# A four-layer network on one core: the last attention layer gets SP-only transfers of eight per half batch, evictions first on ScalarE, two residual buffers and q/k products at the head of TensorE's slots

## The reference

```python
h = ((xg - mu) * rsqrt(var + EPS)).reshape(B, C, N) * norm_w[None, :, None] + norm_b[None, :, None]
qkv = (h.transpose(0, 2, 1) @ qkv_w.T + qkv_b).reshape(B, N, 3, nh, hd)
q, k, v = (qkv[:, :, 0], qkv[:, :, 1], qkv[:, :, 2])
attn = softmax(einsum('bnhd,bngd->bnhg', q, k) * hd ** (-0.5))
o = einsum('bnhg,bngd->bnhd', attn, v).reshape(B, N, C)
return x + (o @ proj_w.T + proj_b).transpose(0, 2, 1)
```

## Time and profile before

| | |
|---|---|
| median of 3 runs | 2309.95 us (2307.72 to 2318.79) |
| the profiled execution's own time | 2301.12 us |
| its span in the trace | 2299.3 us |
| last layer in the trace | about 1810 to 2299 us |
| steady batches 1 to 6 of it | 1868.68 to 2228.66 us |
| granted TensorE clock, whole span | 0.928 |

### The profile page before, as it was taken

The page is one execution under the profiler, slowest core; times in us unless marked ns, Lnnn a source line. Parts: engine busy times, 40 slices in busy tenths (PEclk is TensorE's granted clock), DMA queues, the critical chain, the costliest instruction groups (busy, mean ns, idle before and its releaser), DMA issues.

```text
span 2299.3 us, 36501 instructions
## 1 busy us (share of the span) xinstructions
PE 1999.9 (87%) x12212; PEld 1020.5 (44%) x12212; DVE 1521.9 (66%) x2315; ACT 829.6 (36%) x1546; POOL 1028.1 (45%) x437
## 2 busy tenths in 40 slices
PE   6998786799999999999999999999999777777775
PEld 2443233345544545545545445445543444344442
DVE  6766557787766766767677677677661366666666
ACT  0253220014544544444444444444456222222220
POOL 0242200025543644545455444453546166666666
PEclk7899898789999999999999999999999888889886
DMA  6200020250231232133123213303310201111111
GB/s 212 56 2 0 1 108 8 47 170 12 65 75 42 53 94 49 28 94 75 35 61 75 55 42 75 76 20 75 75 38 2 77 24 61 61 61 61 42 42 58
DMA packets 89410, 132.54 MB, mean 58 GB/s; under 512 B 57925, under 2 KB 58231, under 8 KB 89207
## 3 DMA queue, kind: packets, MB, share of 16 engines
q1 hardware_dynamic: 70486, 128.31, 20.0%
q10 hardware_dynamic: 18720, 1.64, 0.6%
HBM read 44.83 MB, written 25.17 MB: 30 GB/s over the span
## 4 chain that ended last, share of the span: by engine, by line
PE 71%; DVE 13%; issue 4%; ACT 4%; DMA 3%; ACTq 3%; SPq 2%; POOL 1%; POOLq 0%; DVEq 0%
PE AV L636 11%; PE S L623 11%; PE RB L607 11%; PE S L607 5%; PE SUM L646 4%; PE RB L675 4%; PE RB L871 3%; DVE MX L1274 3%; ACTq L1087 3%; PE AV L886 2%; SPq L438 2%; PE RB L922 2%; PE RB L752 2%; PE RB L692 2%; DVE NMH L1282 1%
## 5 line engine op out<-in xcount | busy, mean ns | idle before, releaser
L1274 DVE TENSOR_REDUCE MX<-RB 128x1 f32<-128x512 f32 x783 | 515.1, 684 | 88.5 <-PE RB L607 79.5
L1001 ACT ACTIVATE PR<-S 128x512 f32<-128x512 f32 x640 | 356.3, 597 | 582.3 <-PE S L623 563.0
L1173 POOL TENSOR_TENSOR ACC<-PR 128x1024 f32<-128x1024 f32 x72 | 170.3, 2373 | 761.1 <-ACT PR L1001 759.1
L623 PE MATMUL S<-QS,KS 98*128 98x512 f32 x1152 | 469.8, 459 | 17.5 <-issue 8.3
L1173 POOL TENSOR_TENSOR ACC<-ACC,PR 128x1024 f32<-128x1024 f32 x152 | 360.0, 2372 | 200.3 <-ACT PR L1001 191.7
L607 PE MATMUL RB<-KS,QS 96*128 96x512 f32 x783 | 393.7, 525 | 29.8 <-DVE MX L1274 18.9
L1001 ACT ACTIVATE X<-S 128x512 f32<-128x512 f32 x512 | 283.5, 598 | 281.1 <-PE S L623 273.6
L607 PEld LDWEIGHTS RB<-KS,QS 96*128 96x128 f32 x783 | 245.1, 318 | 249.2 <-DVE MX L1274 151.9
L623 PEld LDWEIGHTS S<-QS,KS 98*128 98x128 f32 x1152 | 221.9, 198 | 218.6 <-issue 93.3
L1274 DVE TENSOR_REDUCE MX<-S 128x1 f32<-128x512 f32 x369 | 251.6, 682 | 32.4 <-PE S L607 27.0
L607 PE MATMUL S<-KS,QS 96*128 96x512 f32 x369 | 186.3, 505 | 12.6 <-DVE MX L1274 8.1
(11 more groups left out here) (234 smaller groups left out, 2114.7 us busy)
## 6 DMA issues: line engine op xcount, KB each, us to landing
X<-out_y SPq DMA_DIRECT2D x32, 1024.0 KB, 4.9
out_y<-X SPq DMA_DIRECT2D x24, 1024.0 KB, 4.1
QS<-HI SPq DMA_DIRECT2D x144, 128.0 KB, 2.5
KS<-HI SPq DMA_DIRECT2D x144, 128.0 KB, 2.5
QS<-LO SPq DMA_DIRECT2D x72, 128.0 KB, 2.5
KS<-LO SPq DMA_DIRECT2D x72, 128.0 KB, 2.5
X<-in_x SPq DMA_DIRECT2D x8, 1024.0 KB, 8.2
WO<-WO ACTq DMA_DIRECT2D x128, 8.0 KB
```

The costliest lines, as they stand in the source:

```text
L623: mm(ST[:, (H * s + h) % BANKS, :], KS[par][:, h, P * mt:P * mt + P], QS[par][:, h, HALF * half:HALF * half + HALF], start=True, stop=True ...
L1001: nc.scalar.activation(exps(i, s, pair)[:, HALF * one:HALF * one + HALF], ST[:, (H * s + h) % BANKS, :], ACT.Exp, scale=1.0 if i is None e ...
L1173: nc.gpsimd.tensor_tensor(ACC[:, pair, :], so_far, exps(i, s, pair), ALU.add).then_inc(pool_used, 1)
L1274: nc.vector.tensor_reduce(out=MX[:, h, t, half:half + 1], in_=bank(), op=ALU.max, axis=AX.X).then_inc(ring_free, 1)
```

## The change

On SP the transfers of a half batch are now eight, with 128 source and 16 target partitions each, and ScalarE starts none; the order of tokens in `scores3` follows. The residual has a second buffer (LATC, memory of the layers before), used in turn, loaded and stored in two transfers each. TensorE runs `front_qk` first in each slot; ScalarE runs `keep_qk`, `keep_o`, `keep_v` first and only then `exp3` and `keep_p`. `group_sums` stands in slots 3 and 5 and `group_stats` in slots 4 and 6 (before: 3 and 4 on both), and GpSimd's `norm_factors` in slot 7 (before: 6).

```diff
-        P_DMAS = 2 * PAIRS
+        P_DMAS = PAIRS
...
+            def load_xres(b):
+
+                for t in range(CT):
+                    load(XRES3[b % 2][t], out_d[b, :, t], xres_in)
+
             sp.wait_ge(y_ready, B)
+            load_xres(1)
             load(out_d[B - 1], XRES, y_out)
             sp.wait_ge(y_out, 16 * B)
-            load(XRES, out_d[0], xres_in)
+            load_xres(0)
...
-                for g in range(PAIRS):
-                    cg, pair = g // PAIRS, g % PAIRS
-                    load(PTK[TOK * g:TOK * g + TOK, st].rearrange("t h j g -> t (h j g)"),
-                         SC[st][64 * cg:64 * cg + 64, pair].rearrange("p j g -> p (j g)"), p_in3)
+                for pair in range(PAIRS):
+                    load(PTK[2 * TOK * pair:2 * TOK * pair + 2 * TOK, st].rearrange("t h j g -> t (h j g)"),
+                         SC[st][:, pair].rearrange("p j g -> p (j g)"), p_in3)
...
                 share(b, 0)
+                if b > 1:
+                    sp.wait_ge(y_out, 16 * (B + CT * (b - 1)))
+                    load_xres(b)
                 share(b, 1)
...
-                        first = P * st + 64 * cg + TOK * pair
+                        first = P * st + 2 * TOK * pair + TOK * cg
...
+                    if b < B - 1:
+                        for unit in FRONT_UNITS[k]:
+                            front_qk(b + 1, unit)
                     if 0 <= n < TILES:
                         transpose3(n)
                     if b > 0 and k in (1, 2, 5, 6):
                         project3(b - 1, k // 4, 0 if k in (1, 5) else 1)
-                    if b < B - 2 and k in (3, 4):
-                        group_sums(k - 3, B + b + 2)
+                    if b < B - 2 and k in (3, 5):
+                        group_sums((k - 3) // 2, B + b + 2)
                     if b < B and k == 3:
                         scores3(b, 1)
                     if b < B - 1:
-                        for unit in FRONT_UNITS[k]:
-                            front_qk(b + 1, unit)
...
-                    if b < B and k in (0, 4) and (b, k) != (0, 0):
-                        exp3(b, k // 4)
-                    if b < B and k in (0 if b == 0 else 1, 5):
-                        share(b, k // 4)
-                    if b < B and k in (3, 7):
-                        keep_p(b, k // 4)
+                    if b < B - 1:
+                        for unit in FRONT_UNITS[k]:
+                            keep_qk(b + 1, unit)
                     if 0 <= n < TILES:
                         keep_o(n)
                     if b < B - 1:
-                        for unit in FRONT_UNITS[k]:
-                            keep_qk(b + 1, unit)
                         keep_v(b + 1, k)
+                    if b < B and k in (0, 4) and (b, k) != (0, 0):
+                        exp3(b, k // 4)
+                    if b < B and k in (3, 7):
+                        keep_p(b, k // 4)
```

More of the change, by code:

```diff
@@ L330, in program @@
                for n in range(2)]
+        XRES3 = [[XRES[:, t] for t in range(CT)], [LATC[t] for t in range(CT)]]
         O3 = [ENC[:, C * n:C * n + C] for n in range(2)]
@@ L545, in share @@
                     sp.wait_ge(p_kept3, 2 * (b - 1) + st + 1)
-                for g in range(PAIRS):
-                    cg, pair = g // PAIRS, g % PAIRS
-                    load(PTK[TOK * g:TOK * g + TOK, st].rearrange("t h j g -> t (h j g)"),
-                         SC[st][64 * cg:64 * cg + 64, pair].rearrange("p j g -> p (j g)"), p_in3)
+                for pair in range(PAIRS):
+                    load(PTK[2 * TOK * pair:2 * TOK * pair + 2 * TOK, st].rearrange("t h j g -> t (h j g)"),
+                         SC[st][:, pair].rearrange("p j g -> p (j g)"), p_in3)
             def store(b):
                 sp.wait_ge(y_ready, B + b + 1)
[L554 to L557, removed]
+                for t in range(CT):
+                    load(out_d[b, :, t], XRES3[b % 2][t], y_out)
             next_xin(1)
@@ L567, in _ @@
             store(B - 1)
-            sp.wait_ge(y_out, 16 * 2 * B)
+            sp.wait_ge(y_out, 16 * (B + CT * B))
         @block.tensor
@@ L1077, in exp3 @@
                                      scale=float(D) ** -0.5).then_inc(e_done3, 1)
[L1079 to L1088, removed]
             def keep_p(b, st):
@@ L1213, in _ @@
                     n = MT * b + k - 3
-                    if b < B - 2 and k == 6:
+                    if b < B - 2 and k == 7:
                         norm_factors(B + b + 2, GNS3, GNB3)
@@ L1620, in residual3 @@
                 if st == 0 and o == 0:
-                    dve.wait_ge(xres_in, 16 * (B + b + 1))
-                cols = super_tile(XRES[:, o, :], st)
+                    dve.wait_ge(xres_in, 16 * (B + CT * max(b + 1, 2)))
+                cols = super_tile(XRES3[b % 2][o], st)
                 nc.vector.scalar_tensor_tensor(out=cols, in0=quarters(src), scalar=BP3[:, o:o + 1], in1=cols,
@@ L1638, in _ @@
                         residual3(b - 1, k // 4, 0 if k in (2, 6) else 1)
-                    if b < B - 2 and k in (3, 4):
-                        group_stats(k - 3, B + b + 2)
+                    if b < B - 2 and k in (4, 6):
+                        group_stats((k - 4) // 2, B + b + 2)
                     if 0 <= n < TILES:
```

## The result

The changed kernel takes 2284.48 us (median of 4 runs, 2280.91 to 2288.11) against 2308.84 (2306.68 to 2318.79) for the kernel before on the same chip: a ratio of 0.9883, with a 95% interval of 0.9838 to 0.9928. It is faster, but by 24 us where 58 were forecast, and lies half a microsecond above the upper end of the range. The profiled execution took 2280.91 us, with a span of 2279.1 and a mean granted clock of 0.923.

What follows compares the result with a forecast made beforehand. Bound: waits in a TensorE–ScalarE loop, with ScalarE's transfer starts on it. Six batches save 53.4 us, batch 0 5, last iterations 2, start costs 2.5: 57.9 off 2301.12 gives 2243, with 8.8 for the median 2252; range 2226 to 2284.

Steps and rivals of the forecast that it cites:

- what the transfers cost on SP: SP's eight transfers a half batch: 7.7 us, or 13.4 if issuing doubles; data wanted 14 and 12.5 us after `weigh`; nothing charged.
- rival C: SP's transfers take three times as long to start and reach GpSimd late: 5 us a batch, 2282 us; chance 0.07.
- D: Rival: q/k units ahead of transposes and projections delay VectorE's projections by 13.7 us a batch, 2392 us; chance 0.05.
- E: Rival: no change, the delays of D and the transfers' gain cancel, 2310 us; chance 0.04.
- `front_v` of slot 0: TensorE's slot 0: waits for `keep_o` behind the group norm, then runs at half clock, charged 2.3 us.
- rival A: Clock doesn't fall at slot 0: `front_v` and a q/k unit give back 2.3 us a batch, 2238 us; chance 0.15.
- the rest of the walk round a batch: Adding up the engines' steps from one `centre` of slot 0 to the next: 51.1 us a batch instead of 60.0.
- slot 4 with its group statistics (0.8): VectorE's slot 4, where `group_stats` now stands: the statistics were charged 0.8 us.
- the bank wait: TensorE's slot 5: `group_sums` waits for the projection's bank until VectorE's residual of slot 6, delaying `front_v` by 1.9 us.
- rival B: Close waits of slots 4, 5 and 6 bring a second half-clock stretch: 3.7 us a batch, 2274 us; chance 0.2.
- `keep_p`: ScalarE's copy between the eviction after slot 7's `front_v` and the group norm, charged 0.2 us.
- the start of the layer: Last layer's start: loading the second residual buffer ahead of layer three's last store costs 2.5 us, bounds 0 and 5.

Runs made afterwards that it cites:

- e7: Kernel before with only the transfers changed: eight from SP, none from ScalarE, old orders and single residual buffer; 2290.55 us, 0.992 of before.
- e14: Changed kernel with `group_sums`, `group_stats` and `norm_factors` back in their old slots; 2244.57 us, 0.9722 of before.
- e8: Kernel before with only the new orders of TensorE's q/k units and ScalarE's evictions, ScalarE still starting transfers; 2316.37 us, 1.0038 of before.
- e10: Changed kernel with `group_stats` working in PSUM and `keep_p` first in ScalarE's slots 3 and 7; 2241.42 us, 0.9687 of before.
- e12: e6 with three tiny VectorE instructions added in slot 1, two with one SBUF input, one with two; 2239.25 us, 0.9689 of before.
- e1: Changed kernel with `group_stats` working in PSUM, so its square has no two SBUF inputs; 2264.64 us, 0.9783 of before.
- e9: Changed kernel with only the second `group_sums` and `group_stats` moved to slot 4; 2255.55 us, 0.9787 of before.
- e2: Changed kernel with `keep_p` first in ScalarE's slots 3 and 7; 2279.79 us, 0.9868 of before.
- e6: Changed kernel with `group_stats` in PSUM, early `keep_p`, late first load of the second residual buffer, second sums and statistics in slot 4; 2213.95 us, 0.957 of before.
- e5: Changed kernel with the second residual buffer's first load issued behind layer three's last store and the next input load; 2274.27 us, 0.9852 of before.
- e13: Kernel before with the second residual buffer alone; 2318.82 us, 1.0029 of before.
- e4: Changed kernel with PSUM `group_stats`, early `keep_p`, `group_sums` ahead of the projection in slot 5, `group_stats` ahead of slot 6's residual; 2255.34 us, 0.9749 of before.

## Why the prediction was right or wrong

**Right in part: what bounded the kernel.** No ACTq row is left in the last layer, and ScalarE's starts were on the path. But the 8.6 us a batch that they had in the chain were not theirs to give back: e7, which removes them alone, gains 0.8%. They paid together with the new orders (e14, 2.8%).

**Right: what the transfers cost on SP.** SP's groups of eight take 5.0 to 6.1 us to start, at the near bound (5.7) and not at twice that, and each lands 1.9 us later (median): rival C did not occur. The rule of the Trainium skill on balancing starts over engines (Perfetto Trace Analysis, DMA Optimizations) did not bind here: no product of GpSimd waited for its data. It was closer than forecast, though. The data were wanted 9.8 and 9.3 us after `weigh`, not 14 and 12.5 (`weigh` of the first half ends at 2051.24, its first product begins at 2061.05), so some 2 us were to spare and not 5. Rivals D and E fell too. D's delay of 13.7 us a batch isn't seen in e8 either, which has the new orders and ScalarE's transfers: its steady batches are no longer than before, and its 0.4% lies in batch 0.

**Right in most batches: `front_v` of slot 0.** In batch 4 it took 2.04 us behind a wait of 2.19, about as charged (2.3 start to start), at a granted clock of 0.50 (columns as above):

```profile
2046.00:2048.00 2.00, 1.93 (x5) 1.51 (x5) 2.00 (x2) 0.00 (x0) 1.66 (x2) 0.50 0.55 104
```

It took 1.86 to 2.04 us in five of batches 1 to 6, but 1.10 in batch 2 behind the same wait of 2.19. So rival A, the full clock, occurred in one batch of six (in two of six in e10), and the forecast's "after just this wait" was not enough to tell the clock.

**Right: the rest of the walk round a batch.** It gave 51.1 us. e10, which has the changed kernel's orders without the hold and the late `keep_p`, measured 50.4, with a bank wait of 1.6 to 2.2 us where 1.9 was forecast. Its batches lie between 47.9 and 53.4, so the agreement to 0.7 us is partly luck.

**Wrong, the step that decides: "slot 4 with its group statistics (0.8)".** The statistics took 5.3 us there. In slot 3 of batches 1 to 5 before, the square took 0.16 while no product ran, but the price in slot 4 depends on what GpSimd does at that moment, and the trace of before held the row that shows it, in batch 0, where the products of GpSimd had already begun:

```profile
1834.98 0.16 DVE L1313 TENSOR_TENSOR DEV<-MV,MG 128x2 f32<-128x2 f32 x1
1835.18 4.80 DVE L1314 TENSOR_TENSOR S<-DEV 128x2 f32<-128x2 f32 x1
```

I costed the instruction by its kind, from the batches where GpSimd stood still. The mechanism is shown by e12: with a product running, an instruction with two inputs in SBUF is held until the product ends, however small it is. The hold is as long as what is left of the product: in batch 0 of the changed kernel the difference met one that ended at 1847.43.

```profile
1845.42 2.04 DVE L1309 TENSOR_TENSOR DEV<-MV,MG 128x2 f32<-128x2 f32 x1
1837.69 9.74 POOL L1200 TENSOR_TENSOR PR<-WO,LO 128x1792 f32<-128x1792 f32 x2 [13.17 <-issue]
```

With one input in SBUF and one in PSUM the instruction isn't held: the square of e1 began 0.07 us behind the product and took 0.17, in each of batches 1 to 5. The difference `DEV<-MV,MG` at 2009.71 also has two SBUF inputs, but it began 0.07 us before the product. VectorE's own products, 0.58 to 0.64 us beside GpSimd's, have one input in PSUM (SUM is there). The Trainium skill (SBUF — State Buffer, Who interferes with whom) states just this: a DVE instruction with two SBUF inputs contends with a GpSimd instruction that reads SBUF, and the one that comes later is blocked for the whole of the other. The trace agrees, with 4.63 to 4.81 us for 0.16. Had I applied that page to the moved instruction, the forecast would have had the hold in it.

**Wrong in size: the bank wait, 1.9 us forecast, 5.9 to 6.3 measured.** Nothing is wrong with its place; it inherits. The residual that frees the bank comes later by the hold, and by the 2.2 us that `keep_p` adds. In e1 (hold gone) the wait is 3.5 us, in e10 (`keep_p` too) 1.6 to 2.2. Behind the longer wait stands the granted clock of 0.50 for `front_v` and a q/k unit, which is rival B's mechanism, in its place of slot 5 but not for its reason of three small waits. Taking the bank wait away (e9) gives 6.4 us a batch although the square still takes 4.74, taking the hold away (e1) 4.1, the late copy (e2) 1.3: 11.8 in sum, and e6 without all three gives 10.4. What rests on one execution each is known to about 2 us a batch, by which equal batches of one trace differ, and by their medians e1 and e9 are equal (0.9783 and 0.9787). So each of hold and bank wait is shown to cost several us a batch; which of them costs more, and how far one hides the other, is not.

**Wrong in size: `keep_p`, 0.2 us on ScalarE.** I charged its own time, not its place behind two evictions, for which VectorE waits 2.23 us. With the hold in place the early copy gives 1.3 us a batch (e2), which is within the scatter; with the hold gone it gives 2.9, and some 22 us by the ratios (e10 against e1).

**Wrong in size: the start of the layer, 2.5 us with bounds 0 and 5; it was 5.8.** I counted the megabyte's transfer alone. The rows of SP:

```profile
1796.75 0.82 SPq L439 DMA_DIRECT2D OHU<-out_y  x2
1797.61 0.43 SPq L439 DMA_DIRECT2D out_y<-X  x1
1807.16 23.47 SPq L439 DMA_DIRECT2D X<-out_y  x4
```

The store goes out right behind the two loads and is done only at the next row, 9.5 us later; before, it took 4.65. The loads delay the store's completion by 4.9 us, twice what I had for their bytes, and the store itself goes out 0.9 us later; VectorE stood idle for 18.02 us before its statistics, 12.27 before. e5 takes that back whole; e13 shows the same 5.9 us from the buffer alone.

**The sum.** In the profiles the gain is 20.2 us of span: the start costs 5.8, batch 0 gives nothing (forecast 5), batches 1 to 5 give 15.3, batch 6 9.5 and the tail 1.8 (forecast 2), and the layers before differ by 0.6. Of the forecast's 8.9 us a batch, 3.1 came in batches 1 to 5, and e10 gets 10.1 with the two causes removed. As a whole e10 took 2241.42 us where 2252 was forecast.

**The parts interact.** Alone the transfers give 0.8%, the orders cost 0.4%, the buffer costs 0.3%; together, without the move of the sums, they give 2.8% (e14). The orders paid only with ScalarE's queue free of transfers. And the move of `group_sums` and `group_stats`, the smallest part by its instructions, costs some 37 us of what the rest gives.

## What to carry to other kernels

Where a change moves a small instruction, look at what the other engines run at its new place, and search the trace for *every* occurrence of that instruction, not for its median: the one batch in which it took 4.80 us in place of 0.16 was the forecast of the new place. A VectorE instruction that is too long for its columns may be held, and what releases it stands in no list of waits; compare its end with GpSimd's, and give it an input in PSUM or move it to where GpSimd stands still. A new wait of x us must be costed against the last engine it hangs on with all that the same change makes that engine late by: it was 1.9 us by itself and 5.9 with the hold and the late copy before it. And a queue's share of the chain is not the time that its removal gives: 8.6 us a batch in the chain, and by e7 at most about 3 in the run.

## What the hardware did that I had not expected

The same wait of 2.19 us before `front_v` of slot 0 was followed by 1.10 us in batch 2 and by 2.04 us in batches 1, 3, 4 and 5 of the changed kernel. And the granted clock fell without a wait of TensorE of a microsecond. In e4, between the scores of slot 3 and `front_v` (same columns as above):

```profile
2009.78 0.34 PE L908 MATMUL S<-X 32*64 32x64 f32 x6 [0.87 <-issue]
2010.04 1.96 PE L893 MATMUL AV<-X 128*128 128x256 f32 x4
```

`front_v` took 1.96 us behind a gap of 0.87 that no instruction explains; the clock was 1.00 from 2008 to 2010 and 0.55 in the two microseconds after. In the other batches from 1 to 5 of e4 it took 1.13 at this place. It may be a part of the 2 us by which equal batches differ. What sets it off was only observed, and stays open. With the hold it is also open whether a shorter GpSimd instruction would be worth its extra start: it wasn't tried.
